# Layer 0's projections written out with four store buffers, and its experts' batch closed directly behind its sums

## What is computed

```python
x = x + attn0(layernorm(x))      # 16 heads of 8, causal, softmax(q k / sqrt(8)) v, then Wo
x = x + ffn0(layernorm(x))       # per batch: the two best of 8 experts (gelu, 128 -> 512 -> 128),
                                 # weighted sum, + input, layer norm with gamma and beta
x = x + attn1(layernorm(x))      # 16 heads, only the best 307 of 1024 keys of each query
x = x + ffn1(layernorm(x))       # gated experts and a shared one
```

## Time and profile before

| what | us |
|---|---|
| median of three runs (3279.27 to 3285.87) | 3282.67 |
| the profiled execution, its time | 3284.45 |
| its span | 3282.7 |
| setup and layer 0's projections, to attention 0's first matmul | 110.3 |
| last product of attention 0, first matmul behind it | 651.4, 671.5 |
| experts, first product to the next stage | 719 to 856 |
| mean granted clock of TensorE, share of full speed | 0.824 |

### The profile page before, as it was taken

One profiled execution on the slowest core, in us unless ns is written; L12 is line 12 of the kernel. 1 busy time (PEld: TensorE's weight loads), 2 busy tenths in 40 slices (PEclk: granted clock), 3 DMA queues, 4 the chain that ended last, 5 costly groups with the idle time before them and its releaser, 6 DMA issues. The chain is left out here.

```text
span 3282.7 us, 73646 instructions
## 1 busy us (share of the span) xinstructions
PE 2569.0 (78%) x23657; PEld 1434.0 (44%) x23705; DVE 2691.4 (82%) x8611; ACT 2390.0 (73%) x3993; POOL 2015.8 (61%) x4527
## 2 busy tenths in 40 slices
PE   3599999849666777877777777776777778779999
PEld 2233333234433544544444444544455445445444
DVE  5788888433649999999999999998999999947444
ACT  2266666624238999999999999998899999943221
POOL 3133333430249999999999999997899999920000
PEclk8699999969766778788777877777777777779999
DMA  5312221001130101101101100110100110010000
GB/s 148 101 45 57 48 54 45 14 21 36 56 83 2 17 4 18 19 2 19 18 2 18 18 10 10 19 17 4 18 8 13 18 16 4 2 34 4 7 7 10
DMA packets 115270, 85.95 MB, mean 26 GB/s; under 512 B 58153, under 2 KB 97339, under 8 KB 114875
## 3 DMA queue, kind: packets, MB, share of 16 engines
q1 hardware_dynamic: 106331, 75.20, 10.5%
q0 software_dynamic: 8192, 4.79, 1.0%
q10 hardware_dynamic: 352, 1.18, 0.1%
HBM read 54.25 MB, written 19.40 MB: 22 GB/s over the span
## 5 line engine op out<-in xcount | busy, mean ns | idle before, releaser
L1391 POOL TENSOR_TENSOR a_near<-a_side,a_z 128x1024 int32<-128x1024 int32 x512 | 968.3, 1891 | 42.7
L1287 PE MATMUL a_ST<-a_qs,a_ks 75*128 75x128 bf16 x4096 | 657.5, 249 | 389.3 <-DVE a_mask L1524 214.0
L1487 DVE MAX8 a_cand<-a_near 128x8 f32<-128x256 f32 x2048 | 810.4, 414 | 0.0
L1287 PEld LDWEIGHTS a_ST<-a_qs,a_ks 75*128 75x128 bf16 x4096 | 458.5, 113 | 556.5 <-DVE a_mask L1524 335.0
L1531 DVE TENSOR_SCALAR_CACHE_REDUCE a_z<-a_S,a_thr 128x1024 f32<-128x1024 f32 x512 | 649.7, 1269 | 14.5 <-POOL a_thr L1367 8.5
L1311 ACT ACTIVATE a_signs<-a_z,a_tiny 128x1024 bf16<-128x1024 f32 x512 | 588.8, 1150 | 75.5 <-DVE a_z L1531 71.9
L1304 ACT ACTIVATE a_signs<-a_S,search 128x1024 bf16<-128x1024 f32 x512 | 570.7, 1115 | 5.3 <-PE a_S L1242 5.2
L1326 ACT ACTIVATE a_eT<-a_ST 128x1024 f32<-128x1024 f32 x512 | 518.7, 1013 | 17.7 <-PE a_ST L1288 17.5
L975 ACT ACTIVATE a_eT<-a_ST 128x512 f32<-128x512 f32 (+3 forms) x768 | 329.2, 489 | 210.4 <-PE a_ST L960 155.1
L1242 PE MATMUL a_S<-a_ks,a_qs 72*128 72x512 bf16 x1024 | 397.7, 478 | 82.2 <-DVE a_z L1531 76.1
L1079 DVE TENSOR_REDUCE a_mx<-a_S 128x1 f32<-128x512 f32 (+3 forms) x768 | 381.1, 547 | 78.0 <-PE a_S L947 68.3
(11 more groups left out here) (365 smaller groups left out, 4410.3 us busy)
## 6 DMA issues: line engine op xcount, KB each, us to landing
a_qs<-q_parts SPq DMA_DIRECT2D x174, 64.0 KB
a_ks<-k_parts SPq DMA_DIRECT2D x174, 64.0 KB
a_qs<-a_flip SPq DMA_DIRECT2D x512, 0.8 KB
q_parts<-p_qp SPq DMA_DIRECT2D x48, 128.0 KB, 1.9
k_parts<-p_kp SPq DMA_DIRECT2D x48, 128.0 KB, 2.1
a_qs<-q_parts SPq DMA_DIRECT2D x60, 96.0 KB
a_ks<-k_parts SPq DMA_DIRECT2D x60, 96.0 KB
f_w<-L_ffn_W SPq DMA_DIRECT2D x16, 256.0 KB, 2.8
```

The lines of the kernel that those rows point to most:

```text
L1287: pe.matmul(ST[:, block_of], ks[:, base(hl) + kb * P:base(hl) + (kb + 1) * P], qs[:, tile(hl):tile(hl) + P], start=True, stop=False)
L1391: pool.tensor_tensor(near[:, hl % NEARS, :].bitcast(I32), side[:, one].bitcast(I32).broadcast_to([P, SEQ]), z[:, hl % H, :].bitcast(I32), ...
L1487: mm = dve.max(found[:, 8 * g:8 * g + 8], near[:, h2 % NEARS, g * SW:(g + 1) * SW])
```

## The change

In `setup` ACT now takes the root of the variances and DVE the reciprocal; the fourth batch's statistics and the aggregates stand ahead of the wait for the sixteen loads, `arrange` behind it. In `project0` the loops are written out. The store buffers (`qp`, `kp`, `vst`) are four instead of two, `xT_ps` two instead of one. The cast of q's rest moves from DVE to ACT (`cast_residue`). q has a semaphore of its own, ahead of k's, and PE transposes chunk n + 1 between chunk n's k and v. The loads of pass 0 move from ACT's queue to SP's, those of pass 1 and the fourth fill behind the barrier into attention 0. In the experts a batch's transposes, statistics and norm follow its sums directly.

```diff
@@ setup
+        @block.scalar
+        def _(act):
+            act.wait_ge(var_s, 1)
+            act.activation(std[:, :], var[:, :], ACT.Sqrt).then_inc(std_s, 1)
...
                 for t in range(b * IB, (b + 1) * IB):
                     dve.bn_stats(bn[:, t, :], k.x[:, t, :])
-                if b == 2:
-                    dve.wait_ge(loaded, 16 * len(loads))
-                    arrange()
             dve.drain()
             for t in range(NT):
                 dve.bn_aggr(mv[:, t, :], bn[:, t, :])
             dve.drain()
+            dve.tensor_scalar(var[:, :], mv[:, :, 1], LN_EPS, None, ALU.add).then_inc(var_s, 1)
             dve.tensor_copy(ln0[0][:, :], mv[:, :, 0])
-            dve.tensor_scalar(ln0[1][:, :], mv[:, :, 1], LN_EPS, None, ALU.add)
+            dve.wait_ge(loaded, 16 * len(loads))
+            arrange()
+            dve.wait_ge(std_s, 1)
+            dve.reciprocal(ln0[1][:, :], std[:, :])
@@ project0, DVE
+            normalize(0)
+            normalize(1)
+            for n in range(NCH):
+                residue(n)
+                if n + 2 < NCH:
+                    normalize(n + 2)
+                add_bias_v(n)
+                last_part(n)
@@ project0, ACT
+            def take_queries(n):
+                act.wait_ge(q_done, n + 1)
+                if n >= 2:
+                    act.wait_ge(qres_s, n - 1)
+                if n >= HELD:
+                    act.wait_ge(stored[n % HELD], STORES * (n // HELD))
...
+            copy_turned(0)
+            for n in range(NCH):
+                take_queries(n)
+                if n + 1 < NCH:
+                    copy_turned(n + 1)
+                take_keys(n)
+                cast_residue(n)
@@ project0, PE
+            turn(0)
+            for n in range(NCH):
+                products(n)
+                if n + 1 < NCH:
+                    turn(n + 1)
+                values(n)
@@ project0, SP (store(n) is one chunk: q's three, v, k's three; CB is 2, HELD 4)
+            fill_pass0(sp, k, 0)
+            for n in range(CB):
+                store(n)
+            fill_pass0(sp, k, 1)
+            store(CB)
+            for n in range(CB):
+                sp.wait_ge(stored[n], STORES)
+            sp.wait_ge(k.blank_s[0], 64)
+            load_pass0(sp, k, 0)
+            for n in range(CB + 1, NCH):
+                store(n)
+            fill_pass0(sp, k, 2)
+            for held in range(HELD):
+                sp.wait_ge(stored[held], STORES * NCH // HELD)
@@ attention0, SP
             load_v(0)
+            sp.wait_ge(k.blank_s[1], 64)
+            load_pass0(sp, k, 1)
             sp.wait_ge(kq_in[0], 16 * DMAS_Q)
+            sp.wait_ge(k.blank_s[2], 64)
             load_pass0(sp, k, 2)
             store_max(0)
+            fill_pass0(sp, k, 3)
+            sp.wait_ge(k.blank_s[3], 64)
             for it in range(ITERS):
                 step(it)
@@ experts0, PE
-                        if m == MS and u == UPS - 1:
-                            turn(NCH - 2)
-                            turn(NCH - 1)
-                        elif m >= 3 and m % 2 == 1 and u in (2, 6):
-                            turn((m - 3) // 2 * CB + (u == 6))
+                        if m >= 2 and m % 2 == 0 and u == 5:
+                            turn((m - 2) // 2 * CB)
+                        if m >= 3 and m % 2 == 1 and u == 2:
+                            turn((m - 3) // 2 * CB + 1)
+                turn(NCH - 1)
@@ experts0, ACT
-                        if m >= 4 and m % 2 == 0 and u == 5:
-                            deviation((m - 4) // 2)
-                deviation(B - 2)
+                        if m >= 3 and m % 2 == 1 and u == 4:
+                            deviation((m - 3) // 2)
                 deviation(B - 1)
@@ experts0, DVE
+                for b in range(B):
                     if 2 * b + 2 < MS:
                         scale(2 * b + 2)
...
+                    lift(CB * b)
+                    add_stats(CB * b)
+                    lift(CB * b + 1)
+                    add_stats(CB * b + 1)
                     if 2 * b + 3 < MS:
                         scale(2 * b + 3)
...
+                    norm_add(CB * b)
+                    norm_add(CB * b + 1)
```

More of the change, by code:

```diff
@@ L112, in build @@
                 k.kq_in = [front.enter_context(nc.semaphore(f"a0_kq_in{c}")) for c in range(2)]
+                k.blank_s = [front.enter_context(nc.semaphore(f"a0_blank{x}")) for x in range(4)]
                 project0(nc, k, ln0)
@@ L248, in project0 @@
 def project0(nc, k, pre):
+    mean, rstd = pre
+    HELD = 4
+    STORES = 16 * (2 * SPLIT + 1)
     with ExitStack() as ctx:
@@ L260, in pair, with four @@
         def pair(make, name, *a):
-            return [make(f"{name}{c}", *a) for c in range(CB)]
-        mean, var = pre
-        std, rstd = sb("std", [P, NT]), sb("rstd", [P, NT])
+            return [make(f"{name}{c}", *a) for c in range(2)]
+        def four(make, name, *a):
+            return [make(f"{name}{c}", *a) for c in range(HELD)]
         xn, xT = pair(sb, "xn", [P, CT, D]), pair(sb, "xT", [D, CW])
@@ L274, in project0 @@
-        qk_done, v_done, q_s, k_s, v_s = (sem(x) for x in ("qk_done", "v_done", "q", "k", "v"))
-        qsplit, ksplit, stored = sem("qsplit"), sem("ksplit"), pair(sem, "stored")
-        blank_s = [sem(f"blank{x}") for x in range(4)]
+        qp, kp = four(sb, "qp", [D, SPLIT, CW], BF16), four(sb, "kp", [D, SPLIT, CW], BF16)
+        vst = four(sb, "vst", [P, CT, D])
+        xT_ps, q_ps, k_ps, v_ps = (pair(ps, x, [P, CW]) for x in ("xT_ps", "q_ps", "k_ps", "v_ps"))
+        xn_s, turned, xT_s = (sem(x) for x in ("xn", "turned", "xT"))
@@ L339, in _, with copy_turned @@
-            project_chunks(0)
-            project_chunks(1)
-            for c in range(CB):
-                act.wait_ge(stored[c], free(1))
-            act.wait_ge(blank_s[0], 64)
-            load_pass0(act, k, 0)
-            project_chunks(2)
-            project_chunks(3)
+            def copy_turned(n):
+                act.wait_ge(turned, n + 1)
+                if n >= 2:
+                    act.wait_ge(v_done, n - 1)
+                act.activation(xT[n % 2][:, :], xT_ps[n % 2][:, :], ACT.Copy).then_inc(xT_s, 1)
@@ new lines, in turn, with products @@
+            def turn(n):
+                pe.wait_ge(xn_s, (n + 1) * CT)
+                if n >= 2:
+                    pe.wait_ge(xT_s, n - 1)
+                for t in range(CT):
+                    mm = pe.transpose(xT_ps[n % 2][:, t * P:(t + 1) * P], xn[n % 2][:, t, :], k.ident[:, :])
+                mm.then_inc(turned, 1)
+            def products(n):
+                c = n % 2
+                pe.wait_ge(xT_s, n + 1)
+                if n >= 2:
+                    pe.wait_ge(q_s, n - 1)
+                pe.matmul(q_ps[c][:, :], k.wq[0][:, :], xT[c][:, :], start=True, stop=True).then_inc(q_done, 1)
+                if n >= 2:
+                    pe.wait_ge(k_s, n - 1)
+                pe.matmul(k_ps[c][:, :], k.wk[0][:, :], xT[c][:, :], start=True, stop=True).then_inc(k_done, 1)
@@ new lines, in values @@
+            def values(n):
+                c = n % 2
+                if n >= 2:
+                    pe.wait_ge(v_s, n - 1)
+                for t in range(CT):
+                    mm = pe.matmul(v_ps[c][:, t * P:(t + 1) * P], xT[c][:, t * P:(t + 1) * P], k.wv[0][:, :], start=True, stop=True)
+                mm.then_inc(v_done, 1)
+            turn(0)
+            for n in range(NCH):
+                products(n)
+                if n + 1 < NCH:
+                    turn(n + 1)
+                values(n)
@@ L406, in fill @@
-            def fill(x):
-                for rows, odd in ((slice(64, P), 0), (slice(0, 64), 1)):
-                    cols = slice((2 * x + odd) * 2 * SEQ, (2 * x + odd + 1) * 2 * SEQ)
-                    for dst, const in ((k.qs, k.fill[0]), (k.ks, k.fill[1])):
-                        sp.dma_start(dst[rows, cols], const[rows, :]).then_inc(blank_s[x], 16)
-            fill(0)
-            store(0)
-            fill(1)
-            store(1)
-            fill(2)
-            store(2)
-            fill(3)
@@ L429, in load_quad, with fill_pass0 @@
+def fill_pass0(queue, k, x):
+    for rows, odd in ((slice(64, P), 0), (slice(0, 64), 1)):
+        cols = slice((2 * x + odd) * 2 * SEQ, (2 * x + odd + 1) * 2 * SEQ)
+        for dst, const in ((k.qs, k.fill[0]), (k.ks, k.fill[1])):
+            queue.dma_start(dst[rows, cols], const[rows, :]).then_inc(k.blank_s[x], 16)
 def load_quad(sp, k, m):
```

180 lines of the change are left out of this document (56 added, 124 removed).

## The result

| | before | after |
|---|---|---|
| median of 4 runs each | 3280.97 us (3278.14 to 3285.87) | 3258.61 us (3257.62 to 3261.69) |
| ratio | | 0.9932 (95% interval 0.9916 to 0.9947) |
| profiled execution (span) | 3284.45 us (3282.7) | 3257.62 us (3255.9) |

What follows compares the result with a forecast made beforehand. No engine bounds the whole span; the first stage and experts are chains timed by their last instruction. Gains of 26.1 us (front) and 5.5 (experts), 31.6 together, gave 3251 us against the median, range 3240 to 3266.

Steps and rivals of the forecast that it cites:

- Setup: Before the projections: work moved under the input wait, first normalized tile at 20.3 instead of 25.8, 5.5 us earlier.
- Chunks: Layer 0's projections: first query store at 31.3, at most 6.0 us a chunk on DVE, second query store ready at 37.
- SP's queue and the start of attention: SP's ordered fills, stores and pass 0's loads end the projections; attention 0 starts at 83.5, 26.8 us earlier.
- Store 2 at 46: In SP's queue in the projections: store 2 done at 46 us, behind fill 1 at 42.5.
- Four buffers: Projections: chunks 4 to 6 need stores 0 to 2, landed long before; only chunk 7 waits, for chunk 3's.
- What is late next: Attention 0's first pass: maxima land behind pass 2's loads at 121, first transposed score 26.1 us earlier, 0.7 given back.
- Experts: Experts' DVE tail: ends at 849.9 instead of 855.37, 5.5 us gained; the extra ACT table switch costs zero.
- A: Front: SP's issue sets the end, attention starts at 77, gain 38.8 us, 3244; chance 0.17.
- B: Front: loads and stores hinder each other as now, attention at 90, 3257, or 3271 at worst; chance 0.22.
- C: Front: work only moves across the barrier, no gain before the first score, 3277; chance 0.05.
- D: Attention 0: late maxima keep TensorE's clock low in the passes, eating the gain or slower, up to 3305; chance 0.04.

Runs made afterwards that it cites:

- fills_first: Changed kernel with all four fills issued by SP at the projections' start and at no other place: 3246.70 us, ratio 0.9893.
- held2: Changed kernel with two store buffers instead of four, and the wait for chunks 0 and 1 before chunk 2's stores: 3264.79 us, ratio 0.9945.
- spread_front: Changed kernel with the loads of passes 0 to 3 alone cut into DMAs of 8 rows: 3252.03 us, ratio 0.9911.
- experts_only: Kernel before with only the change's edits in the experts: 3275.29 us, ratio 0.9977.
- fill2_late: Changed kernel with fill 2 issued behind pass 1's loads instead of at the end of the projections: 3262.64 us, ratio 0.9940.
- max_first: Changed kernel with SP's maxima of pass 0 issued ahead of pass 2's loads instead of behind them: 3272.76 us, ratio 0.9966.

## Why the prediction was right, and where it was off

**Setup: right.** First tile 20.74 for 20.3. The loads landed at 16.83 instead of 16.08 in this execution, which is the difference and more. (The forecast's own terms, 1.04 + 0.35 + 1.24 from 16.08, give 18.71 and not 18.95; a wait of 0.26 us for PE's transposes, which it did not have, came in their place.)

**Chunks: nearly.** First query store 31.95 for 31.3; second 39.16 for 37. The pace on DVE was taken as 6.0 us a chunk at most. The normalization of chunk 3 took 4.64 us for four tiles, where the four before took 1.11, while POOL worked from 30.2 to 37.85 without a pause, and chunk 1's last part of q stands behind it on DVE. The Trainium skill (SBUF — State Buffer, "SBUF: two separate sides") has VectorE and GpSimd share a pair of ports that one of them holds for a whole instruction; the row agrees, and no run here separates it.

**SP's queue and the start of attention: 5.0 us off** (88.48 for 83.5). The step that failed is the price of SP's issues next to a fill, with the pace of the first chunks. "Store 2 at 46" was 52.15, 6.2 us late: 3.0 of this stood already at the end of store 1 (42.5 for 39.5, of which 0.8 is a slip of the forecast, since 37 and a store of 3.3 make 40.3), 0.2 came with fill 1, and 2.9 with store 2, whose issue took 6.4 us for the 3.5 booked, with the 1.05 MB of fill 1 ahead of it in the queue. The loads took 10.3 us, as booked. From their last issue to the end of the stores the forecast had 24.0 us (57 to 81), 6.5 of it for the loads to drain; it took 22.0 (62.55 to 84.57), with one stall, in the keys of chunk 3 (5.10 us for 1.3). So this part was 2.0 us better than forecast. The end was 1.4 worse: fill 2 and the barrier took 3.9 us for 2.5, fill 2 alone 3.2 for "some 2 us". `fills_first` confirms the price: without a fill right ahead of it, store 2 is issued in 3.5 us and done at 48.2, and the start is 5.9 us earlier. The stall in chunk 3's keys stays there (4.44 us) and is gone with 8-row loads: that one is the loads'.

**Four buffers: right in kind.** `held2` gives their part as 6.6 us of the 21.8.

**"What is late next": right in the mechanism, 4.9 us short in size.** The forecast named the maxima behind pass 2's loads and put them 37.5 us after the start; they came at 42.4. The term that was mis-sized is the drain of pass 2's loads, which the forecast had at an even 16.5 us a pass: their tail ran at about 53 GB/s (116 to 120) instead of 76, and one transfer of the maxima took 10.7 us to land behind it, where 1.5 were booked. The fills have a part in it that no run gives alone. Without fill 2 ahead of pass 1's loads and fill 3 behind the maxima (`fills_first`) the longest landing is 5.3 us and the score comes 37.0 us after the start. Fill 3, which the forecast had at nothing, was issued at 120.77 and moved at 211 GB/s between 122 and 127 while PE waited; but in `spread_front` it stands in the same place and the maxima land in 2.3 us. Pass 3's loads and everything later did stay hidden, as forecast.

Two of the signs by which the forecast said it would be right did not come: attention's first score at 82 to 85 (88.5), and the first transposed score 36.8 to 39 us behind it (42.4). The values landed in 4.2 us, within its 3 to 8.

**Experts: 6.3 us for 5.5**, in the trace, and 6.1 in `experts_only`. The pair of tables cost zero. Batch 2's norm starts 105.9 us behind the experts' first product (807.77 less 701.9), where the forecast's chain had 106.7 (825.8 less 719.1), and that is nearly all of the surplus.

**The rivals.** A (SP's issue sets the end, 3244) was half true: the stores of chunk 7 had 3.2 us of fill 2's issue behind them, and moving that away made the start 2.3 us earlier (`fill2_late`); but the engines are 0.90 busy at the stores' 284 GB/s, so the rows do not say which of the two sets 3.5 us a store. (In `fills_first` the engines moved 369 GB/s between 42 and 50, so 284 is not the most they can do.) B (loads and stores hinder each other, 3257) gave the nearest number, and that is luck: it had the start at 90 (88.5) because of 23.2 us for pass 0's loads, which were issued in 10.3 us with one stall of 3.8 behind, and the maxima at 127, where they came at 130.8. C and D did not occur: 16.2 us of the front's 21.8 arrive, and the clock is 0.96 as before.

**What stays open.** What the passes' loads could reach on eight engines: in the 8-row runs SP's issue allows 81 to 88 GB/s, little more than the 81 that they had on three, and no run issues them faster, from two queues for instance. Why a packet of 4 KB took 420 ns there instead of 180 is not shown either. How much of the maxima's delay is fill 2's, how much fill 3's, was not divided. A start with fewer transfers at all, the blanks written by an engine instead of by DMA, was not tried.

## What to carry to other kernels

A small transfer that someone waits for can sit behind everything large that was issued shortly before it and has not drained, so large transfers without inputs (fills, constants) belong in the first stretch where the DMA engines have room, even if a store there is issued later. Moving a late small transfer ahead of large loads is no gain unless the loads' own next user has slack; here it turned 6 us of waiting into 19. Two edits that each gain need not add: before they are combined, see in the trace which wait each of them ended.

## What the runs showed of the hardware that was not expected

- More engines, same rate, smaller backlog: DMAs of 8 rows made the share of the DMA engines 0.52 instead of 0.22 at the same 81 GB/s, with some 420 ns instead of 180 for a 4 KB packet; 36 issues in 14.3 us allow no more. In the steady passes others pay: a gather of denominators that was waited for 0.4 us was waited for 4.1.
- A queue that is full of bytes slows its issuer: three stores that issue in 1.3 us took 3.1 behind a fill and 5.1 behind sixteen loads, and six small ones 9.65 behind loads in `max_first`. Issuing was cheap only while the transfers ahead drained.
- Of six small transfers issued in a row behind a pass's loads the median landed in 2.3 us and the slowest in 10.7 (after); where the loads had drained all six took 1.8 (before).
- The share of the DMA engines is not a share of their best rate: 0.90 at 284 GB/s (after, 70 to 82) and 1.11 at 369 GB/s (`fills_first`, 42 to 50).
- ACT's table load ran at 0.83 us although the root that needs it waited until 14.78.
